# Four attention layers on one core: the scores of two pairs put next to each other in TensorE's order

## The chip, the cores and the metric

The kernel runs on one core of a Trainium2 chip. Time is device time in microseconds (us), from the run's own measurement; the profile adds one execution in which every instruction is recorded. Engines: PE is TensorE (PEld its weight loads), DVE is VectorE, ACT is ScalarE, POOL is GpSimd, SP issues the DMAs.

## The reference, cut to what matters

There are 32 batch rows of x (112 tokens, width 256) and of a context (375 tokens, width 256), in f32. Four layers follow one another. All have cross attention with 16 heads from x to the context; layers 1 and 3 have attention of x to itself first; layers 1, 2 and 3 have a feed-forward part. Layer 1 quantises its operands and the weights of attention.

```python
def layer(x, ctx):                       # 1 and 3; 0 and 2 have no own attention, 0 no feed-forward part
    h = norm(x);  x = x + proj(attention(q=h @ wq, k=h @ wk, v=h @ wv))      # causal in layer 3
    h = norm(x);  x = x + proj(attention(q=h @ wq2, k=ctx @ wk2, v=ctx @ wv2))
    h = norm(x);  return x + ff(h)       # gated gelu in layer 1, relu in 2 and 3

def attention(q, k, v):                  # per batch row and head
    e = exp(q @ k.T * scale - rowmax)
    return (e / e.sum(-1)) @ v
```

## The kernel before

**Streams, octets, pairs.** Two batch rows make a stream (224 token columns), 16 streams a layer. Eight heads of one batch row (own attention: all 16, four to a unit) make an octet. An octet is worked off in pairs of two units: a unit is one head's scores, 112 tokens by 375 context positions (own attention: four blocks of 112 by 112, printed 112x112). A cross octet has 4 pairs, an own octet 2; with 16 cross and 4 own pairs a stream of layer 1 or 3 has 20. There are 1152 pairs.

**What a pair passes through.** TensorE writes the two units' scores into two of four banks of the tile `score` (L948; in layer 3's own attention a matmul with the causal mask comes first, L943). DVE takes the row maxima (L1228). ACT takes the exponential and its row sums (L1119), into one of eight slots of `e`. DVE inverts the sums (L1239, in layer 1 also L1243). POOL multiplies (L1444; in layer 1 L1441 and a second pass, L1451). TensorE transposes the unit (the job `turn`, L960 and L963), ACT or DVE copies the result to `probs` (L1133, L1305), and when an octet's turns are there TensorE multiplies with the values (the job `pv`, L977 to L1004).

**Jobs and the ring.** Everything that TensorE does besides scores is a job that writes one of four banks `ring`: projections of x (`q`, `k`, `v`, `q2`, `o`, `o2`) and of the context (`ck`, `cv`), the feed-forward products (`f1`, `f2`, in layer 1 `gate`, `up`, `f2`), and the sums of a norm (`mean`, `var`, for the context `cvar`). A job waits until the job four before it has been saved by DVE or ACT. A norm goes: `mean` on TensorE, its save on DVE (L1310), squares on ACT (L1086, for the context `csquare`), `var` on TensorE, its save on ACT (L1139, L1142, the "save of var"), the scale on DVE (L1255), the bias on ACT (L1097), and then the products read it. In layer 1 ACT's L1155 rounds and DVE's L1277 and its followers (the `clip`) finish a product.

**What sets the order.** The class `Plan` gives each step a position in units of pairs. The scores of pair p stand at p, its turns at p + 2.35 (2.75 in layer 1, 0.5 more for own attention), other jobs at positions relative to the octets. Sorted by position they are TensorE's order. `arrange` then walks this order with rough costs, and writes from its clock the orders of DVE and ACT: when a maximum, an exponential, an inverse, a save is due, and which of the two engines saves a job. Each engine works off its list in order and waits on semaphores. Scores of pair p wait for the exponentials of pair p - 2 (two banks each), the exponentials of pair p for the turns of pair p - 4.

Of the kernel before, what the change touches and what calls it, by code (L numbers as in the profile page):

```python
# [151 lines left out]
class Plan:  # L152
# [27 lines left out]
    def place_attention(self):  # L180
        for layer in range(4):
            for s in range(STREAMS):
                cross = [(layer, "cross", s, b, half) for b in (2 * s, 2 * s + 1) for half in range(2)]
                if layer in (0, 2):
                    own = [(layer + 1, "self", 0, b, 0) for b in range(2)] if s == STREAMS - 1 else []
                    places = (1, 3)
                else:
                    own = [(layer, "self", s + 1, b, 0) for b in (2 * s + 2, 2 * s + 3)] if s < STREAMS - 1 else []
                    places = (0, 2)
                for at, o in zip(places, own):  # L190
                    cross.insert(at, o)
                for o in cross:
                    self.octet(*o)
        for p in self.pairs:
            lag = 2.35
            if p.octet.layer == 1:
                lag = 2.75
            if p.octet.attn == "self":
                lag += 0.5
            self.steps.append((p.index, "scores", p))  # L200
            for i, u in enumerate(p.units):
                self.job(p.index + lag + 0.1 * i, "turn", p.octet.layer, p.octet.s, p.octet.b, 0, "VA", u)
            if p.index == p.octet.last:
                self.job(p.index + lag + 0.9, "pv", p.octet.layer, p.octet.s, p.octet.b, p.octet.half, "V", p.octet)
# [1385 lines left out]
```

How the kernel before makes its waits and increments, by code:

```python
            def wait_ge(self, semaphore, value):  # L752
                if value > self.met.get(semaphore.num, 0):
                    self.met[semaphore.num] = value
                    self.eng.wait_ge(semaphore, value)
# [1 line left out]
            def saves(self, jobs):  # L757
                for by in "VA":
                    self.wait_ge(saved[by], max([j.nth for j in jobs if j.by == by], default=0))
# [1 line left out]
            def products(self, jobs):  # L761
                if jobs[0].layer == 1 and jobs[0].kind in QUANTISED:
                    self.wait_ge(clipped, max(j.clip for j in jobs))
                else:
                    self.saves(jobs)
# [1 line left out]
            def done(self, jobs):  # L768
                self.wait_ge(job_done, max([j.index for j in jobs], default=-1) + 1)
# [7 lines left out]
        def turned_input(wait, p):  # L777
            if p.octet.layer == 1:
                wait.wait_ge(gridded, grid_count[p])
            else:
                wait.wait_ge(weighed, p.index + 1)
# [1 line left out]
        def normed(wait, n):  # L783
            if n.layer == 0:
                wait.wait_ge(scaled, n.index + 1)
            else:
                wait.wait_ge(biased, biases[n])
# [23 lines left out]
        def scores_done(wait, octets):  # L811
            wait.wait_ge(scored, max([o.last for o in octets], default=-1) + 1)
# [35 lines left out]
        def values_free(wait, layer, user):  # L848
# [1 line left out]
                wait.done(plan.products(user - VS))  # L850
            if layer in (1, 3):
                wait.wait_ge(zeroed, zeros[layer, user % VS])
            if user == 32:
                wait.wait_ge(ctx_scaled, B)
```

## Time and profile before

| | |
|---|---|
| time, median of 3 runs | 5785.81 us (5782.1 to 5785.96) |
| time of the profiled execution | 5777.42 us |
| its span, first to last instruction | 5775.6 us |
| mean granted TensorE clock | 0.931 |
| busy: PE, DVE, ACT, POOL | 91%, 59%, 47%, 44% of the span |
| HBM traffic | 17 GB/s over the span |

A share of the whole span is a mean over four layers with different limits, so the section of rows below goes by stretches. Layer 0 lies at about 20 to 1060 us, layer 1 to 2760, layer 2 to 4460, layer 3 to the end; neighbours overlap by a few pairs. In a timeline a row begins with its start and its length in us; neighbouring instructions of one kind are merged (x4), and what the engine waited for stands in brackets with the idle time. Matmuls are pipelined: a row's length reaches beyond the start of the next, so costs are read from start to start. One f32 product is shown as two matmuls, a bf16 one and a transpose as one.

### The profile page before, as it was taken

How to read it: one execution, taken by the hardware profiler on the slowest of the kernel's cores; microseconds unless marked ns; L12 is line 12 of the kernel's file. 1: busy time of each engine (PE TensorE's matmuls, PEld its weight loads, DVE VectorE, ACT ScalarE, POOL GpSimd, SP SyncE). 2: the span in 40 equal slices, each digit the busy share in tenths (PEclk: the TensorE clock that was granted, in tenths of full speed). 3: DMA queues.
4: the chain of work that ended last, by engine and by line, in shares of the span. 5: the costliest groups of instructions: out<-in, count | busy, mean ns of one | idle time of the engine just before them, and what ended most of it. 6: DMA issues, size and time to landing. Idle time of an engine off the chain costs nothing.

```text
span 5775.6 us, 91653 instructions
## 1 busy us (share of the span) xinstructions
PE 5238.1 (91%) x34496; PEld 3724.5 (64%) x34496; DVE 3404.1 (59%) x7828; ACT 2702.7 (47%) x8497; POOL 2551.6 (44%) x3730
## 2 busy tenths in 40 slices
PE   8999999767767767767999999999999999999999
PEld 5666666455655555555666666666667777777777
DVE  5555555556666666666555455555555666666665
ACT  4555555555555555555332232322334555555554
POOL 2322323788888888889211111111112333333332
PEclk9999999778877877777999999999999999999999
DMA  1000000000000000000000000000000000000000
GB/s 68 18 24 21 18 25 18 33 12 10 9 18 9 9 18 9 9 16 28 31 14 13 12 12 14 11 12 15 12 11 31 26 18 18 18 16 13 18 17 9
DMA packets 39751, 103.09 MB, mean 18 GB/s; under 512 B 4880, under 2 KB 21520, under 8 KB 38032
## 3 DMA queue, kind: packets, MB, share of 16 engines
q1 hardware_dynamic: 39312, 97.23, 5.0%
q8 instruction: 276, 4.52, 0.3%
q14 instruction: 163, 1.34, 0.1%
HBM read 82.53 MB, written 14.68 MB: 17 GB/s over the span
## 4 chain that ended last, share of the span: by engine, by line
PE 74%; POOL 16%; DVE 4%; ACT 3%; issue 2%; DMA 0%; SPq 0%; ACTq 0%; DVEq 0%
PE ring L1013 43%; PE score L948 12%; PE ring L963 11%; POOL e L1451 10%; POOL e L1441 5%; PE ring L995 3%; PE ring L988 3%; DVE nmax L1228 2%; PE ring L1002 1%; ACT e L1119 1%; PE ring L960 1%; POOL e L1444 1%; PE ring L977 1%; DVE probs L1305 1%; ACT heads L1102 0%
## 5 line engine op out<-in xcount | busy, mean ns | idle before, releaser
L1444 POOL TENSOR_SCALAR e<-e,rsum 112x375 f32<-112x375 f32 (+1 forms) x2048 | 1065.7, 536 | 2917.6 <-DVE rsum L1239 2916.0
L1119 ACT ACTIVATE e<-score,nmax 112x375 f32<-112x375 f32 (+1 forms) x2048 | 1041.0, 528 | 649.2 <-DVE nmax L1228 645.5
L1228 DVE TENSOR_REDUCE nmax<-score 112x2 f32<-112x750 f32 (+1 forms) x1152 | 1100.0, 955 | 370.7 <-PE score L948 356.2
L1013 PE MATMUL ring<-h,weights 128*128 128x224 f32 x3840 | 988.8, 389 | 49.9 <-ACT work L1155 28.2
L1451 POOL TENSOR_SCALAR e<-e 112x375 bf16<-112x375 f32 (+1 forms) x640 | 989.9, 1547 | 49.6
L1013 PEld LDWEIGHTS ring<-h,weights 128*128 128x128 f32 x3840 | 725.9, 204 | 207.7 <-issue 46.7
L948 PE MATMUL score<-keys,q 64*112 64x375 f32 (+2 forms) x3584 | 792.8, 508 | 2.7 <-DVE q L1284 1.1
L1133 ACT COPY probs<-ring 125x336 f32<-125x336 f32 (+1 forms) x974 | 409.5, 440 | 820.7 <-PE ring L963 767.6
L1305 DVE COPY probs<-ring 125x336 f32<-125x336 f32 (+3 forms) x1330 | 596.5, 468 | 328.2 <-PE ring L963 216.6
L1119 ACT ACTIVATE e<-score,nmaxc,quant 112x375 f32<-112x375 f32 (+1 forms) x1024 | 554.3, 555 | 410.6 <-DVE nmaxc L1232 408.6
L963 PEld LDWEIGHTS ring<-consts,e 112*125 112x125 f32 x4608 | 597.8, 188 | 209.0 <-issue 128.4
L963 PE MATMUL ring<-consts,e 112*125 112x112 f32 x4608 | 667.3, 279 | 2.7 <-POOL e L1444 2.7
L1013 PE MATMUL ring<-ctx,weights 128*128 128x375 f32 x1536 | 591.9, 509 | 2.5 <-DVE work L1355 2.5
L1441 POOL TENSOR_SCALAR e<-e,rsumw 112x375 f32<-112x375 f32 (+1 forms) x1024 | 483.4, 487 | 225.0 <-DVE rsumw L1243 204.1
L1013 PE MATMUL ring<-weights,ctx 128*125 128x256 f32 (+1 forms) x1536 | 575.9, 506 | 0.0
L948 PEld LDWEIGHTS score<-keys,q 64*112 64x112 f32 (+2 forms) x3584 | 246.5, 166 | 304.5 <-issue 219.8
L1119 ACT ACTIVATION_READ_ACCUMULATOR e<-score,nmax 112x1 f32 x2048 | 438.3, 214 | 0.0
L1013 PE MATMUL ring<-work,weights 128*128 128x224 f32 (+1 forms) x1792 | 406.4, 375 | 3.0 <-DVE work L1264 2.4
L1013 PEld LDWEIGHTS ring<-ctx,weights 128*128 128x128 f32 x1536 | 294.5, 202 | 176.7 <-issue 74.6
L1013 PEld LDWEIGHTS ring<-weights,ctx 128*125 128x125 f32 x1536 | 287.5, 195 | 150.0 <-issue 104.0
L1013 PE MATMUL ring<-heads,weights 128*128 128x224 f32 x1536 | 377.4, 394 | 1.9 <-ACT work L1155 1.1
L1013 PEld LDWEIGHTS ring<-work,weights 128*128 128x128 f32 x1792 | 329.6, 190 | 49.6 <-issue 11.9
(109 smaller groups left out, 5529.4 us busy)
## 6 DMA issues: line engine op xcount, KB each, us to landing
ctx<-ctx_t SPq DMA_DIRECT2D x128, 375.0 KB, 3.0
out_t<-x SPq DMA_DIRECT2D x64, 224.0 KB, 1.9
x<-out_t SPq DMA_DIRECT2D x48, 224.0 KB, 3.3
weights<-weights SPq DMA_DIRECT2D x5, 1024.0 KB, 4.9
x<-x_t SPq DMA_DIRECT2D x16, 224.0 KB, 3.2
weights<-weights SPq DMA_DIRECT2D x1, 3328.0 KB, 11.0
weights<-weights SPq DMA_DIRECT2D x1, 2560.0 KB, 9.1
weights<-weights SPq DMA_DIRECT2D x1, 2304.0 KB, 9.1
```

The costliest lines, as they stand in the source:

```text
L948: ins = pe.matmul(score_bank(u)[0:S, n * width:(n + 1) * width], lhs, rhs, start=not masked, stop=not masked or n == nt - 1)
L963: ins = pe.transpose(dst[0:R, c * S:(c + 1) * S], src[:, c * R:(c + 1) * R], idt[0:S, 0:S])
L988: ins = pe.matmul(ps[64 * odd:64 * odd + 64, 0:4 * S], vs[0:R, c, kv:kv + 64], probs_of(o, c, 4 * odd, 4 * S), start=c == 0, stop=c == last)
L995: ins = pe.matmul(ps[64 * odd:64 * odd + 64, i * S:(i + 1) * S], vs[0:R, c, hd:hd + 64], probs_of(o, c, 4 * odd + i, S), start=c == 0, sto ...
L1013: ins = pe.matmul(out_, a, b_, start=n == 0, stop=n == len(parts) - 1)
L1119: ins = nc.scalar.activation(e_of(u)[:, n * width:(n + 1) * width], score_bank(u)[0:S, n * width:(n + 1) * width], ACT.Exp, bias=minus, sc ...
L1133: ins = nc.scalar.copy(dst, src)
L1228: ins = dve.tensor_reduce(to, src, AX, ALU.max, negate=True)
L1305: ins = dve.tensor_copy(dst, src)
L1441: ins = nc.gpsimd.tensor_scalar(mine, mine, rsumw[0:S, slot(u), n:n + 1], ROUND, ALU.mult, ALU.add)
L1444: ins = nc.gpsimd.tensor_scalar(mine, mine, rsum[0:S, slot(u), n:n + 1], 0.0, ALU.mult, ALU.add)
L1451: ins = nc.gpsimd.tensor_scalar(e_grid(u)[:, 0:full], e_of(u)[:, 0:full], ROUND, 255.0, ALU.subtract, ALU.min)
```

## The change

The second and the fourth pair of an octet get a position 0.98 lower, so that their scores follow the scores of the pair before them. The positions of all other steps stay; the lists of DVE, ACT and POOL are written anew from the new order by the same rules.

```diff
@@ -197,7 +197,8 @@
                 lag = 2.75
             if p.octet.attn == "self":
                 lag += 0.5
-            self.steps.append((p.index, "scores", p))
+            early = 0.98 if (p.index - p.octet.first) % 2 else 0.0
+            self.steps.append((p.index - early, "scores", p))
             for i, u in enumerate(p.units):
                 self.job(p.index + lag + 0.1 * i, "turn", p.octet.layer, p.octet.s, p.octet.b, 0, "VA", u)
             if p.index == p.octet.last:
```

Line numbers of the changed kernel are one higher from there on. Here are three places, each before and then after.

TensorE in layer 0, from the scores of pair 112 on. Here `score<-keys,q` are scores, `ring<-consts,e` the six transposes of a pair's two turns, `ring<-work,weights` the keys from the context (`ck`), `ring<-probs,values` the product with the values. Before:

```order
L948 MATMUL score<-keys,q 112x375 x2
L963 MATMUL ring<-consts,e 125x112 x6
L948 MATMUL score<-keys,q 112x375 x2
L963 MATMUL ring<-consts,e 125x112 x6
L1013 MATMUL ring<-work,weights 128x375 x2
L948 MATMUL score<-keys,q 112x375 x2
L988 MATMUL ring<-probs,values 64x448 x6
L963 MATMUL ring<-consts,e 125x112 x6
```

After:

```order
L949 MATMUL score<-keys,q 112x375 x4
L964 MATMUL ring<-consts,e 125x112 x12
L1014 MATMUL ring<-work,weights 128x375 x2
L949 MATMUL score<-keys,q 112x375 x4
L989 MATMUL ring<-probs,values 64x448 x6
```

The scores of pair 113 moved up to those of 112, and 115 to 114; the transposes of two pairs (110 and 111) now follow one another, with no scores between them.

ACT in layer 1, at the second own-attention octet of a stream (pairs 366 and 367). `e,sums<-score` with 112x112 x8 are the exponentials of one such pair, `squares<-h` the squares of a norm, `rdev` the save of var, `work<-ring` with 128x375 the save of a `ck`, `h<-h` the bias. Before:

```order
L1086 ACTIVATE squares<-h 128x448
L1119 ACTIVATE e,sums<-score,nmaxc,quant 112x112 x8
L1139 ACTIVATE rdev<-ring,eps 128x224
L1142 ACTIVATE rdev<-rdev 128x224
L1155 ACTIVATE work<-ring,magic,quant 128x375
L1097 ACTIVATE h<-h,vectors 128x224 x2
L1119 ACTIVATE e,sums<-score,nmaxc,quant 112x112 x8
L1086 ACTIVATE squares<-h 128x448
```

After:

```order
L1087 ACTIVATE squares<-h 128x448
L1120 ACTIVATE e,sums<-score,nmaxc,quant 112x112 x16
L1140 ACTIVATE rdev<-ring,eps 128x224
L1143 ACTIVATE rdev<-rdev 128x224
L1156 ACTIVATE work<-ring,magic,quant 128x375
L1098 ACTIVATE h<-h,vectors 128x224 x2
```

The exponentials of the second pair moved ahead of the save of var, of the save of ck and of the bias.

ACT in layer 3, at the second own-attention octet of a stream (pairs 922 and 923), with the same names; `probs<-ring` is the copy of a transposed unit. Before:

```order
L1086 ACTIVATE squares<-h 128x448
L1133 COPY probs<-ring 125x3x112
L1139 ACTIVATE rdev<-ring,eps 128x224
L1142 ACTIVATE rdev<-rdev 128x224
L1119 ACTIVATE e,sums<-score,nmax 112x112 x8
L1097 ACTIVATE h<-h,vectors 128x224 x2
L1119 ACTIVATE e,sums<-score,nmax 112x112 x8
```

After:

```order
L1087 ACTIVATE squares<-h 128x448
L1120 ACTIVATE e,sums<-score,nmax 112x112 x8
L1140 ACTIVATE rdev<-ring,eps 128x224
L1143 ACTIVATE rdev<-rdev 128x224
L1120 ACTIVATE e,sums<-score,nmax 112x112 x8
L1098 ACTIVATE h<-h,vectors 128x224 x2
```

The save of var, which stood before both blocks of exponentials, now stands between them, and the bias, which stood between them, now follows both.

## Rows read from the trace of the kernel before

**Rows 1.** The page's slices of the span: granted TensorE clock in tenths

```profile
PEclk9999999778877877777999999999999999999999
```

**Rows 2.** Stretches: length, busy time by engine, clock, DMA

```profile
417.17:479.28 62.11, 62.11 (x325) 39.30 (x324) 35.03 (x70) 32.16 (x95) 18.52 (x32) 1.00 0.06 21
1595.33:1704.53 109.20, 79.38 (x530) 61.44 (x528) 68.57 (x190) 61.69 (x180) 92.19 (x105) 0.78 0.04 12
3451.83:3557.03 105.20, 105.20 (x609) 70.95 (x609) 54.04 (x105) 31.11 (x94) 18.54 (x32) 1.00 0.04 13
4890.82:4895.80 4.98, 4.98 (x22) 3.06 (x21) 3.59 (x7) 1.22 (x4) 3.22 (x9) 0.66 0.00 0
4880.85:4963.48 82.63, 81.13 (x699) 61.55 (x698) 55.44 (x126) 43.26 (x163) 29.51 (x64) 0.98 0.05 16
```

**Rows 3.** TensorE's timeline: start us, length us, instruction, count

```profile
38.53 1.52 PE L948 MATMUL score<-keys,q 64*112 64x375 f32 x8
...
3425.48 0.89 PE L948 MATMUL score<-keys,q 64*112 64x375 f32 x4
3426.30 0.91 PE L963 MATMUL ring<-consts,e 112*125 112x112 f32 x6
3427.04 1.44 PE L1013 MATMUL ring<-ctx,weights 128*128 128x375 f32 x4
3428.32 3.19 PE L1013 MATMUL ring<-heads,weights 128*128 128x224 f32 x16
...
3433.07 1.43 PE L1013 MATMUL ring<-ctx,weights 128*128 128x375 f32 x4
3434.42 0.89 PE L948 MATMUL score<-keys,q 64*112 64x375 f32 x4
```

**Rows 4.** The page's costliest groups: busy us, mean ns, idle before

```profile
L1119 ACT ACTIVATE e<-score,nmax 112x375 f32<-112x375 f32 (+1 forms) x2048 | 1041.0, 528 | 649.2 <-DVE nmax L1228 645.5
...
L1228 DVE TENSOR_REDUCE nmax<-score 112x2 f32<-112x750 f32 (+1 forms) x1152 | 1100.0, 955 | 370.7 <-PE score L948 356.2
...
L1133 ACT COPY probs<-ring 125x336 f32<-125x336 f32 (+1 forms) x974 | 409.5, 440 | 820.7 <-PE ring L963 767.6
...
L1119 ACT ACTIVATION_READ_ACCUMULATOR e<-score,nmax 112x1 f32 x2048 | 438.3, 214 | 0.0
```

**Rows 5.** POOL's timeline in layer 1, first own-attention octet

```profile
1710.39 1.16 POOL L1441 TENSOR_SCALAR e<-e,rsumw 112x375 f32<-112x375 f32 x2 [1.81 <-DVE rsumw L1243]
...
1717.88 2.70 POOL L1441 TENSOR_SCALAR e<-e,rsumw 112x112 f32<-112x112 f32 x8 [3.21 <-DVE rsumw L1243]
```

**Rows 6.** Timelines of layer 1's second own-attention octet: ACT, DVE, PE

```profile
1632.62 0.44 ACT L1119 ACTIVATE e<-score,nmaxc,quant 112x112 f32<-112x112 f32 x1 [0.66 <-DVE nmaxc L1232]
...
1636.01 0.47 ACT L1139 ACTIVATE rdev<-ring,eps 128x224 f32<-128x224 f32 x1
...
1637.78 0.85 ACT L1097 ACTIVATE h<-h,vectors 128x224 f32<-128x224 f32 x2 [0.33 <-DVE h L1255]
...
1639.53 0.44 ACT L1119 ACTIVATE e<-score,nmaxc,quant 112x112 f32<-112x112 f32 x1 [0.89 <-DVE nmaxc L1232]
...
1642.03 0.19 DVE L1239 RECIPROCAL rsum<-sums 112x8 f32<-112x8 f32 x1
...
1636.95 1.02 PE L1013 MATMUL ring<-x,mean_w 128*128 128x224 f32 x4 [0.22 <-ACT rdev L1142]
```

**Rows 7.** TensorE's timeline in layer 1's feed-forward stretch

```profile
1684.07 1.02 PE L1013 MATMUL ring<-h,weights 128*128 128x224 f32 x4 [0.38 <-ACT rdev L1142]
```

**Rows 8.** Timelines of layer 3: PE at the first own-attention octet, ACT and PE at the second

```profile
4889.91 0.98 PE L960 MATMUL ring<-consts,e 112*112 112x112 f32 x8 [1.36 <-POOL e L1444]
...
4905.74 0.34 ACT L1119 ACTIVATE e<-score,nmax 112x112 f32<-112x112 f32 x1
...
4908.38 0.89 ACT L1097 ACTIVATE h<-h,vectors 128x224 f32<-128x224 f32 x2
...
4909.40 0.99 PE L1013 MATMUL ring<-h,weights 128*128 128x224 f32 x4
```

## The prediction

> **What bounds the kernel now.** I read the clock line of the page first: TensorE has its full clock except in a stretch from about 1000 to 2700 us, which is layer 1 [rows 1]. Then the busy time of one stream (two batch rows) per layer. In layers 0 and 2 TensorE is busy for the whole of 62.11 and 105.20 us, so there it never waits and every nanosecond that leaves its list leaves the time. Layer 3 is nearly so, 81.13 of 82.63 us. In layer 1 TensorE is busy 79.4 of 109.2 us, at a mean clock of 0.78, and POOL 92.2 [rows 2]. There POOL's two passes over each pair are the main chain, broken by gaps of 1.81 and 3.21 us while POOL waits for DVE's reciprocals [rows 5], and by a stretch of the feed-forward part where TensorE works almost without a wait [rows 7].
>
> **What the change takes away.** A score matmul uses 64 or 32 rows of the array, the neighbours use all. The rows show what a switch costs. One pair's scores take 0.82 us from start to next start (3425.48 to 3426.30, and again from 3434.42). The four matmuls ahead of a score take 1.35 us (3433.07 to 3434.42) and 1.28 ahead of a full one (3427.04 to 3428.32). So a pair standing alone costs 0.82 + 0.07 = 0.89. At 38.53 two pairs happen to stand together: eight matmuls end 1.52 us after they start, four end after 0.89, so the second pair adds 0.63 [rows 3]. A pair joined to another saves 0.89 - 0.63 = 0.26, with rounding 0.27. Counting the two orders, score groups fall by 128 in layer 0, 96 in layer 2, 97 in layer 3 and 126 in layer 1 (the couples that are left out of this are among the rivals). In the layers that TensorE bounds these are 321 x 0.27 = 87 us, of which layer 3 gives back some 1 us, because 29 of its scores stood next to a product of few columns and no longer do: **-86 us**. Layer 1's 126 are off its chain except in the feed-forward stretch, one or two per stream at about 0.2 us: **-4 us**.
>
> The Trainium skill speaks against part of this: TensorE: Matmul & The Clock Gate, Part 3, "What overlaps and what doesn't", says that weight loads overlap matmuls in flight only where the row groups differ, and the third matmul of a couple uses the first one's rows. By that rule the second pair would cost 0.82 and the saving be only the entry, 321 x 0.08 = 26 us; the one couple in this trace does not agree with it (0.63), and I go by the trace.
>
> **What it adds.** ACT and DVE follow a list that the planner writes, in strict order. With both scores early, both maxima and both exponentials now stand together on these lists. A cross pair's maximum is 0.955 us on DVE; its exponentials are two of 528 ns with two accumulator reads of 214, about 1.3 us; a save of a transposed unit is 0.44 [rows 4]. So after a couple starts, DVE is taken until 0.93 + 2 x 0.95 = 2.8 us and ACT until 1.9 + 2 x 1.3 = 4.5 us. TensorE has four ring banks and must have the save four jobs back.
>
> Layer 0. Take pairs 112 and 113 (the PE rows shown above). Before, scores stood between the two pairs of transposes. Now the couple (1.45 us) is followed by four turns (six transposes take 0.74 us, 3426.30 to 3427.04 [rows 3]) and the ck at 1.45 + 0.07 + 1.4 = 2.9 us. It needs the first turn's save, which ACT does only after exp 112: 3.2 + 0.44 = 3.6. Wait: 0.7 us. The same walk over the other seven couples of a stream gives 0.45 us at pair 103, where a square, an exponential and a csquare stand ahead of the save of var, 0.2 at pair 105, and nothing elsewhere: 1.4 x 16 streams = **+22 us**. In layer 2 (jobs of 1.3 to 1.7 us between) my walk over five couples finds no wait: 0.
>
> Layer 3, second own-attention octet. This is the clearest cost. Its exponentials run 0.33 us apart, 8 of them 2.64 us (4905.74 to 4908.38), and the norm's save of var, then its bias (4908.38, 0.74 to the next), stood before and between them; f1 starts at 4909.40, as soon as that bias is done and with no wait [rows 8]. Now the order is exp, var, exp, bias. Scores at 4901.9; maximum done at 4904.55; exp to 4907.2; var 0.8 to 4908.0; second exp to 4910.6; bias and signal to 4911.5. TensorE would be at f1 at 4909.35. Wait: 2.15 x 15 streams = **+32 us**. In the first such octet the scores of the pair after next wait for the second exponential: I get 1.8 us at that place instead of the 1.36 at 4889.91 [rows 8], which then goes; after it the clock fell to 0.66 for 5 us (4890.82 to 4895.80 [rows 2]). Between -0.6 and +0.4 per stream; I take 0.
>
> Layer 1. DVE's list now has the reciprocal of the pair ahead of the first own-attention octet before the saves that wait for POOL, so the 1.81 us gap goes [rows 5]; the 3.21 one stays (the maximum behind a POOL-released turn still stands ahead of the reciprocal). Against that, at the second octet both exponential blocks stand ahead of the save of var. Before: exp from 1632.62, var at 1636.01, bias 1637.78, the second exp from 1639.53, TensorE's mean released by var at 1636.95, reciprocal at 1642.03 [rows 6]. One block is 3.4 us, so var comes 3.5 us later unless the scores come earlier, and mean, the saves behind it on DVE, and the reciprocal on which POOL waits follow: +2.7 after the walk, with TensorE's list between. In the feed-forward stretch a wait of 0.38 us for var (1684.07 [rows 7]) grows, since a second exp (1.4 us) and its reciprocal stand ahead of ck, var and a save of up: about +1.3. Sum per stream -1.8 + 2.7 + 1.3 = 2.2; x 15 = **+33 us** (bounds -27, where only the closed gap counts, and +60, where nothing is offset).
>
> Clock. New waits may bring the half clock. The row at 4890.82 shows (1 - 0.66) x 5 = 1.7 us lost after a wait of 1.36 [rows 2, 8]; bounds 0 and 1.7 per new wait of that size. I take 1.0 in layer 3 and 0.8 in layer 1's stretch: **+15** and **+12 us**.
>
> DMA: loads and stores keep their data and order and the share is 0.03 to 0.06 [rows 2]; 0.
>
> **Sum.** -86 - 4 + 22 + 32 + 33 + 15 + 12 = +24 us on the profiled execution's 5777.4, so 5801; the three timed runs have a median 8 us above it, so 5809 on their scale. I say 5808.
>
> **Rivals.**
> - *Layer 1 balances itself.* POOL is released earlier by the odd pairs, and the delayed var is hidden because POOL has more pairs in hand. For it: POOL's own work is only 92.2 of 109.2 us [rows 2]. Against: var is in TensorE's list ahead of the turns that POOL feeds. Layer 1 then gives -27 and no clock loss instead of +45: 5808 - 72 = 5736; with half of that, 5770. It decides as soon as layer 1's stream falls below 109.2 us.
> - *No new wait in any layer.* Bought only if ACT's exponentials and reciprocals are never late; then -86 - 4 - 27: 5669. The 2.15 us at f1 speaks strongly against it.
> - *The clock falls with the waits.* In layer 0 too, at the 0.7 us wait: 1.7 x 16 = 27 more, and the full 1.7 in layers 1 and 3: +24. 5808 + 51 = 5859.
> - *The second pair pays its weight load.* The couple at 38.53 is one instance at the program's start. If in the steady state a joined pair costs 0.82, the gain is 26 and not 86: 5868. (That is the skill's rule above.)
> - *The change does nothing:* excluded by the order: 447 of 576 couples are joined there, 32 keep a mask matmul between them and 97 a job.
>
> **How the numbers follow.** The forecast's own case, 5780 to 5835 (layer 0's waits between 0.5 and 2.5 us per stream, layer 1's sum between 1 and 3.5), has 0.48. Layer 1 balancing, 5725 to 5775, has 0.20; no new wait 0.05; clock 0.15; weight load 0.08; other, as more waits in layer 2 or 3 than walked, 0.04. The range 5742 to 5870 leaves out about 2 in 10. 0.2% is 11.6 us and about what can be told from no change. Faster than 5774: nearly all of the second and third cases and 0.04 of the first, 0.28. Within: 0.17, most of it from the first. Slower: 0.55.
>
> **What would show it.** Right: layer 2's stream at about 103.6 us with no wait; layer 0's shorter by 0.8 us with waits for ACT's copy of a transposed unit; in layer 3 f1 waiting some 2 us for ACT's bias once per stream; in layer 1 POOL's 1.81 us gap gone, its gap at the second octet above 3.5, a stream above 109.2. Wrong: a couple's eight matmuls not at 1.5 us, layer 1's stream shorter, or waits in layer 2. The terms in which I trust least are layer 1's and the clock's, since both hang on several queues at once.

## The result

The changed kernel takes 5801.88 us (median of 7 runs, 5799.49 to 5808.46), the kernel before in the same rounds 5785.71 (7 runs). The ratio is 1.003, with a 95% interval of 1.0019 to 1.0042: 16 us slower. Forecast were 5808 (range 5742 to 5870), and slower with 0.55.

The page after. First the granted clock by slices, as [rows 1]; then the section on the chain that ended last, its shares by engine; and, as the last row, the same shares on the page before.

```profile
PEclk9999999777877777777999999999999999999999
...
PE 70%; POOL 12%; ACT 11%; DVE 6%; issue 2%; DMA 0%; SPq 0%; ACTq 0%
...
PE 74%; POOL 16%; DVE 4%; ACT 3%; issue 2%; DMA 0%; SPq 0%; ACTq 0%; DVEq 0%
```

ACT's share of the chain was 3% and is 11%; PE lost 4 points and POOL 4. More of the time now hangs on the engine that runs the exponentials.

Now one stream of each layer, with the columns of [rows 2]: layers 0, 1, 2, 3 in this order, and then two stretches of the layer 3 stream.

```profile
390.68:450.90 60.22, 59.69 (x325) 40.23 (x324) 36.87 (x77) 29.80 (x88) 18.48 (x32) 1.00 0.07 21
1715.32:1829.76 114.44, 77.93 (x529) 60.25 (x528) 66.97 (x191) 61.09 (x179) 91.68 (x104) 0.78 0.04 12
3325.41:3428.11 102.70, 102.70 (x610) 72.02 (x609) 54.39 (x108) 29.73 (x90) 18.52 (x32) 1.00 0.04 13
4894.50:4978.28 83.78, 79.52 (x697) 62.19 (x697) 56.91 (x131) 41.30 (x158) 29.52 (x64) 0.94 0.05 16
4896.50:4904.50 8.00, 7.31 (x71) 5.79 (x72) 3.33 (x9) 2.96 (x12) 6.19 (x17) 0.57 0.01 2
4919.50:4924.50 5.00, 3.88 (x36) 2.22 (x40) 1.38 (x5) 1.44 (x5) 2.71 (x8) 0.66 0.00 0
```

Layer 0's stream fell from 62.11 to 60.22 us, of which TensorE idles 0.53. Layer 2's fell from 105.20 to 102.70 with no wait. Layer 1's rose by 5 us at the same mean clock, 0.78, with TensorE busy less than before. Layer 3's clock is 0.94, and falls twice in a stream.

The layers' sums in the two profiled executions, from the starts of their first cross-attention scores (before: 1064.7, 2765.7, 4472.8; after: 1041.2, 2810.3, 4477.8) and the ends of the spans:

| | layer 0 | layer 1 | layer 2 | layer 3 | sum |
|---|---|---|---|---|---|
| forecast, us | -13 | +41 | -26 | +22 | +24 |
| measured, us | -23 | +68 | -40 | +20 | +25 |

So the sum was met because the terms erred both ways; that it came within 1 us is luck. TensorE's timeline after, at a couple of layer 2, the place that answers to [rows 3]:

```profile
3428.11 1.52 PE L949 MATMUL score<-keys,q 64*112 64x375 f32 x8
3429.56 0.91 PE L964 MATMUL ring<-consts,e 112*125 112x112 f32 x6
3430.30 1.44 PE L1014 MATMUL ring<-ctx,weights 128*128 128x375 f32 x4
```

Eight matmuls end after 1.52 us, as the one couple at the start of [rows 3] had it, and the next work starts after 1.45; the transposes behind it take 0.74 to the next start, as they did behind a single pair. TensorE's timeline in layer 3, at the places of [rows 8]:

```profile
4897.19 1.59 PE L949 MATMUL score<-keys,q 32*112 32x375 f32 x4 [1.81 <-ACT e L1120]
...
4904.70 0.90 PE L949 MATMUL score<-keys,q 32*112 32x375 f32 x8
4905.53 0.65 PE L1014 MATMUL ring<-heads,weights 128*128 128x224 f32 x2
...
4920.62 1.83 PE L1014 MATMUL ring<-h,weights 128*128 128x224 f32 x4 [2.17 <-ACT h L1098]
```

The wait of f1 for the bias is there, 2.17 us (forecast 2.15), and the wait of the scores, 1.81 (forecast 1.8). What I had not seen: the couple at 4904.70 ends 0.90 us after its start, no later than four matmuls alone in layer 3 before (0.89 from 4899.58). TensorE's waits in layer 3 from 4560 to 5600 us (line, releaser: total us, times, longest), 13 streams:

```profile
PE ring L1014 <- ACT h L1098: 28.1, 13, 2.2
PE score L949 <- ACT e L1120: 25.8, 26, 1.8
```

In layer 1 POOL is read, since its passes are the main chain there. Here are its first pass of a pair and the gap ahead of it, before, at four places of one stream ([rows 5] has the last two places, one stream earlier); the first row is the second own-attention octet, the last the first octet of the next stream:

```profile
1751.80 2.70 POOL L1441 TENSOR_SCALAR e<-e,rsumw 112x112 f32<-112x112 f32 x8 [3.50 <-DVE rsumw L1243]
...
1813.29 1.16 POOL L1441 TENSOR_SCALAR e<-e,rsumw 112x375 f32<-112x375 f32 x2 [0.47 <-DVE rsumw L1243]
...
1819.59 1.16 POOL L1441 TENSOR_SCALAR e<-e,rsumw 112x375 f32<-112x375 f32 x2 [1.81 <-DVE rsumw L1243]
...
1827.08 2.70 POOL L1441 TENSOR_SCALAR e<-e,rsumw 112x112 f32<-112x112 f32 x8 [3.21 <-DVE rsumw L1243]
```

The same four places after; the third has no gap worth a bracket any more:

```profile
1755.95 2.71 POOL L1442 TENSOR_SCALAR e<-e,rsumw 112x112 f32<-112x112 f32 x8 [6.42 <-DVE rsumw L1244]
...
1820.12 1.16 POOL L1442 TENSOR_SCALAR e<-e,rsumw 112x375 f32<-112x375 f32 x2 [3.21 <-DVE rsumw L1244]
...
1833.65 2.71 POOL L1442 TENSOR_SCALAR e<-e,rsumw 112x112 f32<-112x112 f32 x8 [4.82 <-DVE rsumw L1244]
```

The second octet's gap grew by 2.92 us. The gaps at and ahead of the first octet were 0.47 + 1.81 + 3.21 = 5.49 and are 3.21 + 4.82 = 8.03, so the gap that closed came back elsewhere. What stands behind the 6.42, from the timelines of PE and DVE at the same place (before: [rows 6]):

```profile
1750.97 1.86 PE L1014 MATMUL ring<-x,mean_w 128*128 128x224 f32 x4 [3.98 <-ACT rdev L1143]
...
1755.39 0.19 DVE L1240 RECIPROCAL rsum<-sums 112x8 f32<-112x8 f32 x1
```

TensorE's mean waited 0.22 us for the save of var [rows 6] and waits 3.98; the bias follows on ACT, then the gate product, the transpose behind it, its save, and only then the reciprocal that POOL waits for.

### The profile page after: what moved, and what is told of

It is laid out like the page before. It is cut to its first block, busy times and chain, and to the rows that moved or that the text cites. A ratio compares the mean times of both kernels' runs of the same rounds, so it can differ in the third digit from the quotient of the medians.

```text
span 5800.7 us, 91934 instructions
## 1 busy us (share of the span) xinstructions
PE 5117.0 (88%) x34496; PEld 3762.0 (65%) x34496; DVE 3433.0 (59%) x8088; ACT 2611.6 (45%) x8237; POOL 2543.7 (44%) x3730
## 4 chain that ended last, share of the span: by engine, by line
PE 70%; POOL 12%; ACT 11%; DVE 6%; issue 2%; DMA 0%; SPq 0%; ACTq 0%
PE ring L1014 42%; PE score L949 10%; PE ring L964 9%; ACT e L1120 8%; POOL e L1452 7%; POOL e L1442 4%; PE ring L996 3%; PE ring L989 3%; DVE nmax L1229 2%; PE ring L1003 2%; PE ring L961 1%; ACT work L1156 1%; PE ring L978 1%; DVE probs L1306 0%; ACT heads L1103 0%
## 5 line engine op out<-in xcount | busy, mean ns | idle before, releaser
L1229 DVE TENSOR_REDUCE nmax<-score 112x2 f32<-112x750 f32 (+1 forms) x1152 | 1075.4, 951 | 327.9 <-PE score L949 314.3
L1014 PE MATMUL ring<-h,weights 128*128 128x224 f32 x3840 | 975.9, 386 | 103.2 <-ACT work L1156 43.9
L1134 ACT COPY probs<-ring 125x336 f32<-125x336 f32 (+3 forms) x829 | 359.1, 442 | 1024.4 <-PE ring L964 952.0
L1306 DVE COPY probs<-ring 125x336 f32<-125x336 f32 (+3 forms) x1475 | 652.7, 465 | 224.5 <-PE ring L961 109.2
L949 PE MATMUL score<-keys,q 64*112 64x375 f32 (+2 forms) x3584 | 648.2, 512 | 34.7 <-ACT e L1120 31.3
L1372 DVE COPY values<-ring 125x512 f32<-125x512 f32 (+2 forms) x414 | 202.8, 512 | 292.0 <-PE ring L1014 291.0
```

The lines of the kernel that those rows point to most:

```text
L949: ins = pe.matmul(score_bank(u)[0:S, n * width:(n + 1) * width], lhs, rhs, start=not masked, stop=not masked or n == nt - 1)
L1014: ins = pe.matmul(out_, a, b_, start=n == 0, stop=n == len(parts) - 1)
L1134: ins = nc.scalar.copy(dst, src)
L1229: ins = dve.tensor_reduce(to, src, AX, ALU.max, negate=True)
L1306: ins = dve.tensor_copy(dst, src)
L1372: ins = dve.tensor_copy(dst, src)
```

## The experiments

Each kernel is the changed one with the edit shown; e1 alone is the kernel before with its edit. For every one I worked out from its trace the length of a stream in each layer, from the first cross-attention scores of one stream to those of the next, the mean over the twelve from the start of stream 2 to that of stream 14 (the first is stream 0). These agree within 0.01 us between kernels in layers 0 and 2 where nothing differs, so they tell a layer's part apart better than a total does. A time with "(one)" is a single run.

| kernel | time, us | ratio (95%) | layer 0 | layer 1 | layer 2 | layer 3 |
|---|---|---|---|---|---|---|
| before | | 1 | 62.11 | 109.2 | 105.20 | 81.6 |
| the change | 5801.88 | 1.003 (1.0019, 1.0042) | 60.22 | 114.3 | 102.70 | 83.4 |
| e1 lists kept | 5888.39 | 1.02 (1.0187, 1.0213) | 60.22 | 111.4 | 102.70 | 91.9 |
| e2 layer 2 only | 5736.32 | 0.9928 (0.9915, 0.9941) | 62.11 | 109.2 | 102.70 | 81.5 |
| e3 layer 1 only | 5852.39 | 1.0128 (1.0115, 1.0141) | 62.11 | 114.4 | 105.20 | 81.6 |
| e4 layer 3 only | 5801.85 | 1.0032 (1.0019, 1.0045) | 62.11 | 109.2 | 105.20 | 83.6 |
| e5 cross only | 5707.19 | 0.9879 (0.9862, 0.9895) | 60.23 | 110.9 | 102.70 | 80.2 |
| e6 first own octet | 5788.91 (one) | | 62.11 | 109.2 | 105.20 | 81.8 |
| e7 second own octet | 5887.59 (one) | | 62.11 | 112.7 | 105.20 | 85.1 |
| e8 late exponential | 5745.94 (one) | | 60.23 | 112.7 | 102.70 | 80.8 |
| e9 layers 0, 2, 3 | 5694.66 | 0.9854 (0.9841, 0.9868) | 60.22 | 109.3 | 102.70 | 80.5 |
| e10 close couples | 5686.32 | 0.9842 (0.9828, 0.9855) | 60.22 | 109.2 | 102.32 | 80.3 |
| e11 behind the bias | 5693.31 (one) | | 60.23 | 109.3 | 102.70 | 80.8 |
| e12 same rows | 5718.22 (one) | | 60.22 | 109.2 | 102.70 | 82.3 |

The kernel before had a median of 5778.05 us beside e1 to e4, 5774.84 beside e5 to e8, 5777.92 beside e9 to e11, and 5774.07 in the one run beside e12.

**e1, the lists of before.** TensorE's order is the change's, in all layers; the planner writes the other engines' lists from the old positions.

```diff
         self.arrange()
+        move = lambda k, x: 0.98 if k == "scores" and (x.index - x.octet.first) % 2 else 0.0
+        self.tensor = [(k, x) for _, k, x in sorted(self.steps, key=lambda s: s[0] - move(s[1], s[2]))]
```

> TensorE's order as in the change, in all layers; the lists of DVE, ACT, POOL and SP are those of the kernel before. Theory (the joined scores gain, the regrouped lists of DVE and ACT lose): the gain of the joins stays and the losses of layers 1 and 3 go. Layer 2's stream fell by 2.5 us for 6 joins, 0.4 us a join, so 321 joins x 0.4 = 128 us less than before, with at most some 20 us of ring waits in layer 0: 5660 to 5680 us, and layer 1's stream at 109 or less. Rival (the early scores themselves push TensorE's other work, and its clock, late): layers 1 and 3 keep their losses (+5.1 and +1.6 us a stream), 5790 to 5805 us. Halfway, about 5730, would say that both have a part.

Measured: 5888.39 us, 110 more than before, where my theory said 100 or more less and its rival 5790 to 5805; both missed. (The profiled execution was the slowest of the four, 5909.64.) The loss lies in layer 3. TensorE's waits there, in the stretch of the waits shown above, and then one stream:

```profile
PE score L950 <- ACT e L1121: 42.7, 57, 1.8
PE ring L1015 <- ACT h L1099: 17.6, 12, 1.5
PE score L945 <- ACT e L1121: 11.9, 11, 1.1
...
4901.80:4994.00 92.20, 84.72 (x699) 64.79 (x698) 53.93 (x127) 43.81 (x163) 29.80 (x64) 0.93 0.05 15
```

The scores of pair p need the banks of pair p - 2, and with the old list the second pair's exponentials stand where they stood, behind saves that are now later than its scores. The couple after it then waits. So in layer 3 the lists have to move with the scores: the banks ask for it. These waits are not the whole loss. TensorE idles 92.20 - 84.72 = 7.48 us in this stream, 3.2 more than in the change's, and is also busy 5.2 us longer; a wait between the two pairs of a couple parts them, and I have not divided those 5.2 us between that and the clock. Layer 1 says the reverse: its stream is 111.4 and not 114.3, so there 2.9 of the 5.1 us lost do come from the new lists. Layers 0 and 2 are as in the change to 0.01 us, so there it makes no difference which of the two sets of lists is used.

**e2, e3, e4, one layer each.** One condition is added, with 2, 1 or 3:

```diff
-            early = 0.98 if (p.index - p.octet.first) % 2 else 0.0
+            early = 0.98 if (p.index - p.octet.first) % 2 and p.octet.layer == 2 else 0.0
```

> The change in layer 2 alone. Both theories: no wait of TensorE appears there, and 16 streams gain 2.5 us each, so 5786 - 40 = 5746 us. If a join were worth the 0.27 us of my sum, 5786 - 96 x 0.27 = 5760. Under 5755 is for the larger join.

> The change in layer 1 alone. Theory that layer 1's loss is its own (its second own-attention octet's lists and the reciprocals behind them): 15 streams x 5.1 us plus the ends, 5786 + 77 = 5863 us, stream at 114.3. Rival (a part of it came in from layer 0 and its clock): below 5830.

> The change in layer 3 alone. Theory: two waits of about 2 us per stream, one at f1 and one at the scores of the first own-attention octet, against 6 joins of 0.4 us and one wait of 1.4 us that goes: +1.6 us a stream, 5786 + 25 = 5811 us. Rival (layer 3's loss came from the state in which layer 2 left the clock): no slower than 5786.

Measured against before in the same rounds: -42, +74 and +24 us. TensorE's busy time in layer 2 over 1450 us of e2, with the columns of [rows 2]:

```profile
2900.00:4350.00 1450.00, 1450.00 (x8619) 1018.99 (x8619) 767.81 (x1529) 424.50 (x1304) 262.55 (x461) 1.00 0.04 14
```

It never waits, and six joins a stream bring 2.50 us: 0.42 a join and not 0.27. Layer 1's loss is its own: +74 us for the 77 expected. Layer 3's loss, 24 us for 25, appears with layer 2 as before, so it needs no state of the clock that a changed layer 2 would leave.

But e4's median hides something. Ten of its twelve runs took 5800.77 to 5803.46 us at a mean granted clock of 0.920 or 0.921; the other two took 5766.95 and 5767.56 at 0.928 and 0.927, which is 11 us faster than before. The program is the same. So layer 3's loss goes with the clock: with less time at the lower level, the same joins and waits come out ahead of the kernel before. Neither of the two shorter executions was profiled, and why they kept more of the clock is open. All seven runs of the whole change lie near its median.

**e5, e6, e7, which octets.** The condition is `p.octet.attn == "cross"` in e5, and own attention with `p.octet.b % 2 == 0` (e6) or 1 (e7).

> The second pair's scores stand early in the cross-attention octets of all layers; the own-attention octets keep the order of before. Theory (layer 3's two waits and most of layer 1's loss come from the own-attention couples): layer 3 keeps 6 joins a stream and none of the new waits, 81.5 - 6 x 0.4 = 79.1 us a stream; in layer 1 only POOL's gaps between cross pairs change, which add up to +1.3 us in the trace of after, so 110.5. Sum against before: layer 0 -30, layer 2 -42, layer 3 -37, layer 1 +20, together about -89 us. Rival (the loss is in ACT's and DVE's grouping for any couple): layer 3 at 81 or more, layer 1 at 112 or more, sum -30 or less.

> Only the first own-attention octet of each stream of layers 1 and 3 has its second pair's scores early. Theory: POOL's gap before this octet in layer 1 goes from 3.21 to 4.8 us, so 109.2 + 1.6 = 110.8 us a stream there; layer 3 has a wait of 1.8 us for the exponential in place of one of 1.4, so 81.5 to 82.0. Rival (layer 1's loss is a knock-on of the cross couples): no change, 109.2.

> Only the second own-attention octet of each stream of layers 1 and 3 has its second pair's scores early. Theory: POOL's gap before this octet in layer 1 goes from 3.50 to 6.4 us, so 109.2 + 2.9 = 112.1 us a stream; in layer 3 the wait of 2.2 us at f1 appears, and with it the clock falls, so 81.5 + 2.2 + 1 = 84 to 85. Rival for layer 3 (f1's wait needs the delay of the first octet ahead of it): 82 or less.

e5 came out 68 us faster and not 89. Layer 1 is at 110.9 (expected 110.5). Layer 3 is at 80.2 and not 79.1, since waits for exponentials do not go with the own-attention couples. TensorE's waits from 4560 to 5600 us in e5:

```profile
PE score L949 <- ACT e L1120: 36.2, 39, 1.8
```

So the 1.8 us wait belongs to the first cross couple behind an own-attention octet, whose second scores need the banks of that octet's second pair. What did go is f1's wait. Two streams of layer 3 in e5:

```profile
4757.27:4836.70 79.43, 75.63 (x697) 59.55 (x697) 56.15 (x126) 43.49 (x163) 29.07 (x64) 1.00 0.06 17
4836.70:4917.75 81.05, 77.25 (x697) 60.92 (x697) 56.33 (x126) 43.50 (x163) 29.09 (x64) 0.98 0.06 17
```

e6 missed, and its rival was right: POOL's gap before the first octet grows to 5.04 us, but the 1.81 one ahead of it closes, and the stream stays at 109.2. Joined own-attention scores there cost layer 1 nothing a stream by themselves. (Its one run is still 14 us above before; some 4 us of that stand ahead of layer 1's first cross-attention scores and the rest is spread over layers 1 and 3.) e7 hit: layer 1 at 112.7 (112.1 expected), layer 3 at 85.1 (84 to 85), slower than the whole change, as the cross joins are missing. Three successive streams of e7 price a fall of the clock, since the work in them is the same:

```profile
4874.25:4959.25 85.00, 81.30 (x697) 61.74 (x697) 55.65 (x127) 42.99 (x162) 29.27 (x64) 0.98 0.05 16
4959.25:5047.36 88.11, 84.42 (x696) 63.89 (x696) 55.77 (x127) 42.98 (x162) 29.27 (x64) 0.94 0.05 15
5047.36:5130.80 83.44, 79.73 (x697) 60.48 (x697) 56.03 (x127) 42.98 (x162) 29.40 (x64) 1.00 0.05 16
```

TensorE's busy time is 79.73, 81.30 and 84.42 us, that is 1.57 and three times 1.56 over the least. In the 88.11 us stream the clock is low at two places, and the second costs twice the first: its mean is 0.66 over 4964.25 to 4969.25, 0.57 over 4984.25 to 4989.25 and 0.74 over 4989.25 to 4994.25. Layer 1's parts, cross couples +1.7, second octet +3.5, first octet 0, add up to 5.2 of the 5.1 us lost.

**e8, the second pair's exponentials later.** Only the place on ACT's list changes.

```diff
-                rest.append((exp_at, "A", 4.4 if own else 1.3, "exp", x))
+                late = 2.0 if own and x.index != x.octet.first and x.octet.layer in (1, 3) else 0.0
+                rest.append((exp_at + late, "A", 4.4 if own else 1.3, "exp", x))
```

> The whole change, but on ACT's list the exponentials of the second pair of each own-attention octet in layers 1 and 3 stand behind the saves that were due between them (save of var and of ck, and in layer 3 the bias; at the first octet of layer 1 the save of cv). Theory (the second exponential block ahead of these saves makes the loss): in layer 1 POOL's gaps of 6.4 and 4.8 us go back to about 3.9 and 3.2, so 114.3 - 4.1 = 110.2 us a stream; in layer 3 f1 waits less than 0.5 us instead of 2.2, but the scores of the pair after next wait up to 1.6 us for the late exponential, so 83.6 - 1 = 82.5 us. Rival (the maxima on DVE or the joined scores themselves delay var): gaps above 6, stream 113 or more.

In layer 1 the gap at the first octet went back to 3.21 us, as expected, and the one at the second did not, so the stream is 112.7 and not 110.2. POOL and TensorE in e8:

```profile
1741.61 2.70 POOL L1443 TENSOR_SCALAR e<-e,rsumw 112x112 f32<-112x112 f32 x8 [6.39 <-DVE rsumw L1245]
...
1738.57 1.83 PE L1015 MATMUL ring<-h,weights 128*128 128x224 f32 x4 [2.86 <-ACT h L1099]
```

Mean no longer waits for var, but the exponential block now stands ahead of the bias, and the gate product waits 2.86 us for that. Layer 3, where this edit does put the block behind the bias, lost f1's wait, and with it most falls of the clock:

```profile
4783.53:4863.21 79.68, 75.89 (x696) 59.56 (x696) 57.56 (x131) 41.53 (x158) 29.07 (x64) 1.00 0.06 17
4863.21:4944.51 81.30, 77.50 (x697) 61.02 (x697) 57.71 (x131) 41.54 (x158) 29.10 (x64) 0.98 0.06 17
```

That makes 80.8 us on the mean, below the 82.5 expected. Of the 2.6 us gained on the change, some 2.2 are TensorE's busy time, at a clock of 0.98 to 1.00 for 0.94, and only 0.5 is idle time, since other waits of up to 0.8 us came in place of f1's. The feared wait of the scores behind the late exponentials is no longer than in the cross-only kernel (35.9 us in 39 waits).

**e11, behind the bias in layer 1 too.** `late` is 2.6. At the first octet of layer 1 one more save of a transposed unit comes ahead of the block (the planner takes it from DVE's list for ACT's). The orders of TensorE and POOL are those of e8 and of the change.

> As the late-exponential kernel, but in layer 1 too the second pair's exponentials stand behind the norm's bias. In that kernel the bias was still behind them: TensorE's gate product waited 2.9 us for it, and POOL's gap at the second own-attention octet stayed at 6.4 us. Theory (POOL waits for the reciprocal, that for the save of a transposed unit, that for TensorE past the gate, that for the bias, that for the second exponential block): the gap goes to 3.5 to 4.0 us and layer 1's stream from 112.5 to 109.9 to 110.3 us; layer 3 as there, 80.8 on the mean; total 5746 - 38 = 5708. Rival (the two maxima on DVE delay the reciprocal): gap above 5.5, stream above 112.

POOL at the second octet:

```profile
1716.05 2.70 POOL L1443 TENSOR_SCALAR e<-e,rsumw 112x112 f32<-112x112 f32 x8 [2.52 <-DVE rsumw L1245]
```

The gap is 2.52 us, less than before the change, layer 1's stream is 109.3 and the kernel takes 5693.31. That is the whole of the 5.1 us back with every couple still joined, and more than expected (a gap of 3.5 to 4.0, a stream of 109.9 to 110.3, 5708 us). The rival of the two maxima falls: they stand together here too.

**e9 and e10, what is left when layer 1 is spared.** e9's condition is `p.octet.layer != 1 and (p.octet.layer != 3 or p.octet.attn == "cross")`; e10 has the same condition and moves by 0.9999 and not 0.98.

> The change where it was seen to gain: layers 0 and 2 in full, layer 3 in its cross-attention octets, layer 1 as before. Theory (the layers add up): the cross-only kernel, whose layer 1 took 110.9 us a stream on the mean, less 1.7 us x 15 streams = 26, so 0.9879 x 5775 - 26 = 5680 us, ratio 0.983 to 0.985. Rival (layer 1's earlier starts feed into the layers behind it): above 5700.

> As the kernel of layers 0, 2 and 3, but a second pair's scores move ahead by 0.9999 of a place and not 0.98, so that one more couple of each stream of layer 2 stands together (9 groups of scores a stream and not 10). If a join in layer 2 is worth 2.5 / 6 = 0.42 us: 102.70 - 0.42 = 102.3 us a stream, 7 us in all; if 0.27 as in my sum: 102.4; if a wait comes with it, 102.7 or more. Which shows on the streams, not on the total.

e9 is 83 us faster than before, e10 92, the fastest kernel of the study. e9 missed its 5680 by 15 us. Layer 1's stream is as expected (109.3), but from first scores to first scores the layer took 1704 us against e5's 1720, 16 less and not 26. A good part of the rest is at the ends: the stream before the last is shorter in e5 (93.7 us against 96.8), and so is the first (104.5 against 105.9). The one more couple of e10 is worth 0.38 us a stream of layer 2. The intervals of the two ratios overlap, but e10's five runs in the same rounds (5686.14 to 5689.52) all lie below e9's four (5690.44 to 5695.28). A stream of layer 2 in e10:

```profile
3355.00:3457.32 102.32, 102.32 (x610) 72.19 (x608) 54.47 (x110) 29.45 (x89) 18.48 (x32) 1.00 0.04 13
```

**e12, both pairs on the same rows.** To learn why layer 3's couples are so cheap. The edit is made to e9, whose condition it has too.

```diff
-            rows = slice(32 * (u.k % 4), 32 * (u.k % 4) + 32)
+            lane = u.k % 2 if o.layer == 3 and not is_own(o) else u.k % 4
+            rows = slice(32 * lane, 32 * lane + 32)
```

> As the kernel of layers 0, 2 and 3, but in layer 3's cross attention both pairs of a couple read their 32 rows from the same two row groups, rows 0 to 63 (so the scores of half of the heads are computed from the wrong rows; the work is of the same size). In that kernel a couple's eight matmuls end 0.90 us after they start, no later than four do alone (0.89), with rows 0 to 127 in use. Theory (a layer 3 pair fills two of four row groups and the second pair runs beside it): the couple takes about 1.5 us, as with the 64-row matmuls of layer 0, 0.6 us more for each of 5 couples a stream: layer 3's stream at 83 to 83.5 us on the mean instead of 80.5, 5730 to 5740 us in all. Rival (layer 3's couples are cheap for another reason, as the wait ahead of them): eight matmuls still at 0.9 us, and 5690 to 5697.

A couple in e9, and what follows it:

```profile
4830.32 0.90 PE L949 MATMUL score<-keys,q 32*112 32x375 f32 x8
4831.15 1.02 PE L1014 MATMUL ring<-heads,weights 128*128 128x224 f32 x4
```

The same couple in e12:

```profile
4834.73 1.52 PE L950 MATMUL score<-keys,q 32*112 32x375 f32 x8
4836.17 1.02 PE L1015 MATMUL ring<-heads,weights 128*128 128x224 f32 x4
```

And a stream of layer 3 in e12:

```profile
4827.49:4909.37 81.88, 78.10 (x697) 60.95 (x697) 56.63 (x126) 43.42 (x163) 29.07 (x64) 1.00 0.05 17
```

From start to next start 0.83 became 1.44. Against the streams of e5 at the same clock, whose layer 3 is the same, TensorE is busy 78.10 - 75.63 = 2.47 us longer, which is four couples of 0.61. I had expected five; the fifth is split by its wait. The total rose by 24 us over e9's and not by 35 to 45, since most of these streams kept the full clock; e12 and the kernel before were run once each there.

## Why the prediction was right, and where its terms were not

The direction was right for the stated reason: new waits behind ACT's exponentials, with the clock falls that come with them in layer 3, cost more than the joins save. The size was luck, as layers 1 and 3 show below. Of the signs that were named, layer 2's stream came to 102.70 us and not 103.6, and layer 0's is shorter by 1.9 us and not by 0.8.

**What the change takes away.** The couple's length was right (1.52 us, nearly everywhere in layers 0 and 2), and with it the rival in which the second pair pays its weight load is gone: it adds 0.63 us (1.45 - 0.82), not 0.82. The rule of the Trainium skill in TensorE: Matmul & The Clock Gate, Part 3, "What overlaps and what doesn't", that weight loads overlap matmuls in flight only where the row groups differ, would have made it 0.82 as the prediction read it; the trace does not agree. But 0.27 a join was too low: 0.42 in layer 2 and, by TensorE's busy time, (62.11 - 59.69) / 8 = 0.30 in layer 0. I had counted what a lone pair costs before and in itself, and not what it costs behind: the transposes after scores take 0.74 us to the next start [rows 3]. TensorE's timeline before, further on in the same stretch, has them behind a full product:

```profile
3436.10 0.81 PE L963 MATMUL ring<-consts,e 112*125 112x112 f32 x6
3436.75 1.89 PE L1013 MATMUL ring<-weights,ctx 128*125 128x512 f32 x4
```

That is 0.65, so 0.09 is another part, and 0.27 + 0.09 = 0.36 lies between the two layers' values. Why these differ from each other I have not settled. In layer 3 the step failed: I took layer 0's couple for a couple of 32-row matmuls. There a pair fills two of four row groups and the next pair the other two, and the second pair costs nothing (0.90 against 0.89; e12: 1.52 on the same rows). TensorE's busy time in a stream at full clock fell from 79.63 us to 75.89 (e8, shown there), 3.7 and not 1.7. The row before:

```profile
4805.25:4886.38 81.13, 79.63 (x696) 60.47 (x697) 55.33 (x126) 43.26 (x163) 29.51 (x64) 1.00 0.05 16
```

With the rows shared, in e12 (cross-attention couples alone), it is 78.10, which is 1.5 less than before and near the 1.7. The Trainium skill has this in TensorE: Matmul & The Clock Gate, "Why this matters for your kernels": matmuls on slices of 32 partitions that land in distinct row groups run at the same time. The trace agrees (0.90 us for eight, 0.89 for four), and I had not weighed it.

**Layer 0's waits.** Forecast 1.4 us a stream; TensorE idles 0.53. Of the three waits walked, the one for ACT's copy of a transposed unit, at the stream's first couple, is there (0.50 us for 0.7), and the other two are not. The term was 22 us and measured 8.

**Layer 3's waits.** Both were right in place and size (2.17 and 1.81 us). I balanced the second against the 1.36 us wait that went and booked 0. In all a stream idles 83.78 - 79.52 = 4.26 us and not 1.5 [rows 2], so +2.8 for 2.15. And e5 shows that the 1.81 is not the own-attention couple's, as the prediction had it, but the first cross couple's.

**Layer 1.** The term for the second octet was right: +2.7 forecast, +2.92 measured, and e11 shows the cause, the place of one exponential block. The step that failed is "so the 1.81 us gap goes [rows 5]; the 3.21 one stays". The first did go, but the gap ahead of it grew from 0.47 to 3.21 and the one behind from 3.21 to 4.82: +2.5 for -1.8. The second of these is ACT's block ahead of the save of cv (e8: 3.21 again). The first comes with the cross couples (3.24 us in e5, where the own-attention ones are not joined); I have not followed its chain. In the feed-forward stretch, on the other hand, POOL's gaps came out even (over seven pairs 4.06 us before and 4.28 after, +0.2 for my +1.3). In all POOL's gaps grew by 2.9 + 2.5 + 0.2 = 5.7 us, and its busy time fell by 0.5 (92.19 to 91.68), which is the 5.2 us that this stream grew, where the forecast had 2.2 and 0.8 for the clock.

**Clock.** Layer 1's mean did not change, 0.78 and 0.78, where I had booked 12 us. Nor does its stream follow the clock there, with POOL as the main chain. e9 has layer 1 as before; one of its streams is

```profile
1688.84:1798.30 109.46, 78.09 (x529) 60.06 (x528) 68.50 (x190) 61.53 (x182) 92.05 (x104) 0.80 0.04 12
```

that is 1.3 us less busy time on TensorE than before at a clock of 0.80, and no shorter. Layer 3's was under-booked: TensorE's busy time in a stream of the change is 79.52 at 0.94, and 75.89 in e8 at 1.00 with the same joins, 3.6 us; before, one stream in three had a fall of 1.5 [rows 2]. So +3.1 a stream for my +1.0. The price of one fall was right (1.57 us in e7, upper bound 1.7), their number was not.

**The sums.** Layer 3: -3.7 + 2.8 + 3.1 = +2.2 a stream, the 2.2 that the change's 83.8 us stream shows against 81.6 (the mean of twelve is 83.4). An error of 2.0 one way and of 2.8 the other nearly cancelled there, by luck; and e4's two runs at 5767 us suggest that the 3.1 of the clock is not the same in every run of a kernel. Layer 1 was 27 us too low, layers 0 and 2 together 24 too high. The forecast's direction rests on what was right: that the waits behind ACT's exponentials, with the clock falls at them, outweigh the joins. That is shown by e11, which moves the second exponential blocks of the own-attention octets back on ACT's list and turns 16 us slower into 85 us faster (one run, 5693.31 against a median of 5777.92); layers 1 and 3 each gain by it.

## What to carry to other kernels

When scores are joined on TensorE, look where the second block of exponentials falls on the strict list of the engine that runs it: put it behind the norm's short steps, on which TensorE waits. Here that turned a loss of 16 us into a gain of 85. Before pricing small matmuls side by side, look which rows of the array each uses; two pairs on different row groups cost as much as one. And judge a change that is made in all layers layer by layer: here -23, +68, -40 and +20 us hid in +25.

## What the runs showed of the hardware

- A matmul pair of 32 rows placed beside one on the other two row groups adds 0.01 us (0.90 for 0.89), on the same groups 0.63 (1.52).
- A fall of TensorE's clock to its lower level costs 1.57 us of TensorE's busy time in a stream of layer 3, and streams of the same work pay for none, one or three (83.44, 85.00 and 88.11 us in e7). In the changed kernel it falls at the 1.81 us wait that ends at 4897.19 and at the 2.17 one that ends at 4920.62 (means of 0.57 and 0.66 over the stretches shown), in e5 in every second stream though the waits are the same in all, and in e12, with the longer couples, in none from the layer's fifth stream on. Whole executions differ too: e4 took 5801 to 5803 us at a mean clock of 0.921 in ten runs and 5767 at 0.928 in two. What decides it I can't say from these runs.
